# One core, a fused convolution and selective scan: a carry column is added one scan ahead of its use instead of two

## What is computed

```python
def step(h, inp):
    dt_t, B_t, C_t, x_t = inp
    dA = jnp.exp(dt_t[..., None] * A)
    dBx = dt_t[..., None] * B_t[:, None, :] * x_t[..., None]
    h = dA * h + dBx
    y = jnp.einsum('bdn,bn->bd', h, C_t)
    return (h, y)
```

## Time and profile before

| what | us |
|---|---|
| median of 3 runs | 13839.43 (13836.56 to 13845.37) |
| the profiled execution | 13837.79 |
| its span, first to last instruction | 13836.0 |
| VectorE busy | 13466.6 (97%) |
| GpSimd busy | 13246.6 (96%) |
| ScalarE busy | 12104.2 (87%) |
| TensorE busy | 10079.9 (73%) |

### The profile page before, as it was taken

How to read it: one execution, slowest core, us unless ns; L and a number is a source line. 1 busy time by engine, 2 the same in 40 slices (tenths; PEclk the granted TensorE clock), 3 DMA queues, 4 the chain that set the end, 5 groups by cost and what they waited for, 6 DMA issues and landing times.

```text
span 13836.0 us, 170380 instructions
## 1 busy us (share of the span) xinstructions
PE 10079.9 (73%) x34752; PEld 2897.7 (21%) x34752; DVE 13466.6 (97%) x12084; ACT 12104.2 (87%) x24809; POOL 13246.6 (96%) x3076
## 2 busy tenths in 40 slices
PE   6777777777777777777777777777777777777776
PEld 1222222222222222222222222222222222222221
DVE  7999999999999999999999999999999999999999
ACT  7888888888888888888988888888898888888888
POOL 6999999999999999999999999999999999999999
PEclk8888888888888888888878888788888888888887
DMA  6667676666766676666667666666666666666665
GB/s 146 161 154 161 155 163 156 158 157 157 164 156 160 152 163 158 160 157 156 158 159 164 153 163 151 163 159 156 161 153 163 156 161 156 160 156 163 158 155 128
DMA packets 1195180, 2175.99 MB, mean 157 GB/s; under 512 B 152321, under 2 KB 161594, under 8 KB 1194042
## 3 DMA queue, kind: packets, MB, share of 16 engines
q1 hardware_dynamic: 1192762, 2164.07, 66.7%
q10 hardware_dynamic: 1280, 0.02, 0.0%
HBM read 1811.17 MB, written 352.32 MB: 156 GB/s over the span
## 4 chain that ended last, share of the span: by engine, by line
POOL 53%; issue 32%; DVE 6%; ACT 5%; PE 1%; DMA 1%; SPq 0%; POOLq 0%; ACTq 0%; DVEq 0%
POOL hq L1064 38%; POOL dbx L1054 15%; DVE hq L946 4%; ACT ps_a L640 2%; DVE dbx L929 1%; ACT dbx L654 1%; DMA b_rep<-bc_d 0%; DMA dt_d<-dt 0%; DVE pp L905 0%; ACT xh L600 0%; ACT L600 0%; ACT L765 0%; PE ps_acc L456 0%; DMA dtx_d<-sp 0%; POOLq L1063 0%
## 5 line engine op out<-in xcount | busy, mean ns | idle before, releaser
L1064 POOL TENSOR_TENSOR hq<-hq,c_rep 128x2048 f32<-128x2048 f32 x2048 | 9251.0, 4535 | 468.8 <-ACT carry L659 465.0
L946 DVE TENSOR_TENSOR_SCAN hq<-ps_a,dbx 128x512 f32<-128x512 f32 x8192 | 9443.6, 1207 | 128.8 <-ACT dbx L654 47.2
L640 ACT ACTIVATE ps_a<-dt_rep,A_neg 128x512 f32<-128x512 f32 x8192 | 5625.2, 687 | 1294.7 <-DVE hq L946 1231.5
L1054 POOL TENSOR_TENSOR dbx<-dtx_rep,b_rep 128x2048 f32<-128x2048 f32 (+1 forms) x1024 | 4082.1, 3986 | 99.1 <-DMA dtx_rep<-dtx_d 89.1
L654 ACT ACTIVATE dbx<-ps_a,dbx,carry 128x1 f32<-128x1 f32 x7168 | 2504.9, 349 | 240.2 <-POOL dbx L1054 140.4
L929 DVE TENSOR_TENSOR dbx<-dtx_rep,ps_b 128x2048 f32<-128x2048 f32 (+1 forms) x1280 | 2626.7, 2052 | 9.5 <-PE ps_b L444 9.3
L456 PE MATMUL ps_acc<-hq,dsum 128*32 128x512 f32 x16384 | 2334.0, 643 | 292.6 <-POOL hq L1064 292.6
L382 PE MATMUL pp<-sq,w_b1T 128*128 128x512 f32 x512 | 531.1, 1141 | 1608.7 <-ACT sq L579 1608.7
L444 PE MATMUL ps_b<-dbl,bsel 41*128 41x512 f32 x2560 | 1587.3, 703 | 153.3 <-DVE dbx L929 97.7
L400 PE MATMUL pp<-x,W_taps 128*128 128x512 f32 x768 | 693.3, 1002 | 895.2 <-DVE x L900 531.4
L456 PEld LDWEIGHTS ps_acc<-hq,dsum 128*32 128x32 f32 x16384 | 355.9, 111 | 1865.7 <-issue 1046.5
(11 more groups left out here) (123 smaller groups left out, 10466.4 us busy)
## 6 DMA issues: line engine op xcount, KB each, us to landing
dtx_rep<-dtx_d SPq DMA_DIRECT2D x2048, 256.0 KB, 5.4
dt_rep<-dt_d SPq DMA_DIRECT2D x2048, 256.0 KB, 6.3
c_rep<-bc_d SPq DMA_DIRECT2D x1024, 256.0 KB, 4.7
xr<-in_x SPq DMA_DIRECT2D x704, 256.0 KB, 10.9
b_rep<-bc_d SPq DMA_DIRECT2D x2048, 64.0 KB, 5.5
dtx_d<-sp SPq DMA_DIRECT2D x256, 512.0 KB, 2.8
dt_d<-dt SPq DMA_DIRECT2D x256, 512.0 KB, 6.1
xin<-in_x SPq DMA_DIRECT2D x256, 256.0 KB, 10.2
```

Of the source, the lines that this page charges most:

```text
L640: A(ps_a[:, BANK[i], :], dt_rep[:, q // NQ, g, :], ACT.Exp, scale=A_neg[:, q // NQ, q % NQ, g:g + 1]).then_inc(exp_done, 1)
L946: v.tensor_tensor_scan(hq[:, q % HQ, g, :], ps_a[:, BANK[i], :], dbx[:, slot(q), g, :], 0.0, ALU.mult, ALU.add).then_inc(scan_done, 1)
L1054: g.tensor_tensor(dbx[:, slot(q), m:, :], dtx_rep[:, d, m:, :], b_rep[:, q % NQ // 2, :].unsqueeze(1).to_broadcast([P, DG - m, T]), ALU.mu ...
L1064: g.tensor_tensor(quad, quad, c_rep[:, c % 2, q % NQ, :].unsqueeze(1).to_broadcast([P, DG, T]), ALU.mult).then_inc(cmul_done, 1)
```

## The change

The step at which each tile's carry is added becomes a list that is worked out once. For the first tile of the odd groups (tiles 4, 12, 20 and 28, whose product GpSimd makes, of tile 12 a part of the group) it is step i-1, and for all others step i-2 as before. So in steps 3, 11, 19 and 27 two carries stand next to each other, and in steps 2, 10, 18 and 26 there is none. Tile 8 stays in the burst of step 5. The adds themselves and their waits are the same.

```diff
+IN_BURST = ACT_XZ + 3
+ADD_AT = [[i for i in range(2, NT + 2) if i != IN_BURST and u == (i - 1 if i % (2 * DG) == DG else i - 2)] for u in range(NT)]
 BY_DVE = (0, 2, 3, 4, 6)
...
-                    if u + 2 < NT:
-                        if c % CH and u != ACT_XZ + 1:
-                            add_carry(b, c, u + 2)
-                    elif c + 1 < end and (c + 1) % CH:
-                        add_carry(b, c + 1, u + 2 - NT)
+                    for i in ADD_AT[u]:
+                        if i < NT:
+                            if c % CH:
+                                add_carry(b, c, i)
+                        elif c + 1 < end and (c + 1) % CH:
+                            add_carry(b, c + 1, i - NT)
...
                         if c % CH:
-                            add_carry(b, c, u + 3)
+                            add_carry(b, c, IN_BURST)
```

## The result

The changed kernel takes 14191.1 us (median of 4 runs, 14190.6 to 14197.0), the kernel before 13839.5 us. The ratio is 1.0255, 95% interval 1.0237 to 1.0272: **352 us slower**. The forecast was 14190.

The account below looks back on a forecast made before the run. VectorE, with almost no slack, was taken as the bound. Seven chunks at 1.1 us plus tile 12's 0.89, 3 x 0.39 and 3 x 0.41 gave 11.0 us an image, 352 us over 32 images: 14190 us, range 14090 to 14290.

Parts of the forecast that it names:

- The bound: Whole kernel: VectorE busy 97% of the span, under half a microsecond slack per chunk, so waits before scans lengthen it almost one for one.
- Tile 4, a dead heat: Step 3: carry 4 ready 1.00 us after scan 2 ends, scan 4 due at 1.06 us, so cost nil.
- Tile 12: Carry behind decay 13 and any `pool_part`: 0.89 us lost in chunk 1, 0.39 in chunks 2 to 4, 0.41 in 5 to 7.
- What comes back in chunks 2 to 4: ScalarE, no longer held at tile 4, is 0.50 us sooner; taken off tile 12's loss, leaving 0.39 us each.
- GpSimd's extra room hides nothing: Whole kernel: GpSimd's added time in longer chunks saves nothing, since scans would not wait for it.
- Tiles 20 and 28: Carries behind `evac_conv` and `square`: scan 20 loses 0.88 us, scan 26 regains 0.20; together 1.1 us a chunk.
- The pitch of the scans: VectorE scans without a wait follow each other by 1.13 us, though each shows 1.20 us.
- The waits: VectorE's waits for `add_carry` grow from 123 (47.2 us) to some 670, by about 300 us.
- Nothing is regained: Rival, chance 0.08: each place pays its own delay in full, 15.6 us an image, 14337 us.
- A new wait for GpSimd: Rival, chance 0.08: later `keep_carry` delays GpSimd's product for the next odd group, 86 us on top, 14276 us.
- Faster: Rival, chance 0.04: ScalarE no longer stands still before a late GpSimd product with decay i+1 queued behind; 13783 us.
- My bound of 56 us: Most that rival "Faster" could gain: VectorE's 47.2 us of waits for `add_carry` plus 9 us uncounted idle time.

## Why the prediction was right, and where it was not

*The bound.* VectorE without slack, so that a delay ahead of a scan counts almost one for one: right. Its busy time is the same to 6 us, and the chunks grew by what their scans came late, less what waits further on swallowed.

*Tile 4, a dead heat.* Right in chunks 1 to 5 and 7: scan 4 loses 0.02 us or less. Wrong in chunk 6, which the sum left out: ScalarE comes late out of chunk 5 there, the carry had a lead of 0.35 us and not the 1.03 us of chunks 1 and 5, and scan 4 loses 0.19 us.

*Tile 12.* With `pool_part` scan 12 was forecast 1.12 us late, 0.89 us net of what scan 13 wins back, from a chunk whose lead was small (0.14 us; the average of chunk 1 is 0.27). Averaged over the images it is 1.00 us in chunk 1 and 0.9 us net. That the net figure is met is luck: in the very chunk of the rows it is 0.91 us and 0.7 net, and scan 9 had already won back 0.20 us there. In chunks 5 to 7 scan 12 loses 0.30 to 0.33 us for the 0.41 forecast. With tile 12 alone moved, chunk 6 does lose 0.41; in the changed kernel the carry of tile 4 is out of the way too, and that alone raises the lead at tile 12 of chunk 6 from 0.23 to 0.34 us.

*What comes back in chunks 2 to 4.* The mechanism is right, but the term was taken from one image. I took off 0.50 us. In that image chunk 2 wins back 0.53 us at scans 4, 9, 13 and 17, and grew by 1.50 us for the 1.49 forecast. The average is 0.8 us and 1.23 us, since in nine of the 32 images chunk 2 wins back 1.3 to 1.5 us, most of it at scan 9 (0.76 us) and scan 17 (0.45 us). There VectorE had waited for TensorE's sum in its product `y` and for ScalarE in its softplus instruction. Of 48 and 20 such waits in the whole kernel one each is left, at the very end and the very beginning of the span:

```profile
DVE y L916 <- PE ps_acc L456: 29.3, 48, 10.2
...
DVE pp L905 <- ACT sp L620: 21.3, 20, 15.3
```

```profile
DVE y L919 <- PE ps_acc L458: 10.2, 1, 10.2
...
DVE pp L908 <- ACT sp L622: 15.0, 1, 15.0
```

Why it is these images isn't shown. The sentence that GpSimd's extra room hides nothing was wrong for chunks 2 to 4: with tile 20 or 28 alone moved this room halves ScalarE's wait for GpSimd, and scans start sooner for it.

*Tiles 20 and 28.* 0.90 us at scan 20 for 0.88, and 0.49 us at scan 28 for the 0.46 that is 1.13 less 0.67; scans 22 to 27 win back 0.2 to 0.3 us. Chunks 4 and 5 are not as I took them. In chunk 4 the place costs 0.79 us at scan 28: two instructions of the attention stand ahead of the carry in step 25, and its lead was 0.05 us and not 0.35. In chunk 5 it costs 0.80 us, with a lead of 0.21, and scans 22 to 27 win back 0.54, because four small instructions of the attention had held scan 27. I had counted none of these.

*The pitch of the scans.* The 1.13 us for scans without a wait was read at scan 21 of the earlier trace rows, which the same paragraph reads as waiting for its carry. In the trace the commonest pitch of two scans is 1.11 us; the slip is under 0.02 us for a scan and changes no term by more than 0.03 us.

So the sum came out at 11.0 us for an image where 11.1 were measured, but that it is so close is in part luck: terms of +0.2 us each (chunks 4 and 6) and -0.3 us (chunk 2) cancel in it, and in chunk 5 two of 0.3 us. Tile 20 and, outside chunks 4 and 5, tile 28 were good to 0.03 us, tile 12 in chunks 1 and 5 to 7 to 0.1, the return in chunk 2 to 0.3, the sum by chunk to 0.3, and only the total to 0.1.

*The waits.* VectorE's waits were forecast at about 350 us and are 453: I gave the net loss, where the table counts the waits and not what is regained behind them.

*The rivals.* "Nothing is regained" (14337 us) fell: it would have been right only if scans 26 and 9 had not been waiting already. "A new wait for GpSimd" fell: its product is late 3 times in the changed kernel, 2.4 us in all, and its waits for `keep_carry`, longer by 329 us, held up no scan. "Faster" was the true mechanism at one place of four, worth 44 us by itself. My bound of 56 us held, but not by its working: it counted waits for a carry alone, and these gave 9 us.

## What to carry to other kernels

In this kernel a carry came as late as all that stood between it and its scan in ScalarE's order, so "one step later" is no unit: before a carry is moved, list what the steps that it crosses hold, by pitch and not by duration, and set that against its lead over its reader. Move it only where the lead is larger or where the wait that it gets out of the way is longer; here that was one tile of four. Work the sum out on more than one image when the chunks of the kernel before differ from image to image. And where several engines are nearly full, look which is next: here ScalarE's gain at tile 4 ended at 0.3%, with GpSimd and VectorE both busy for more than 99% of chunk 3.

## What the runs showed that was not expected

Pitch, and not duration, decided each place. With sums of durations tile 20's carry would have come 0.68 + 0.58 = 1.26 us behind the start of decay 21, and tile 28's 1.94 us behind that of decay 28; measured were 1.09 and 1.70. The idle time in front of a scan is short by the overlap of two scans, 0.07 to 0.09 us: scan 20 starts 0.90 us later and shows 0.81 us idle.

A longer chunk is in part its own remedy: each of the three moves that made the kernel slower also shortened ScalarE's waits for GpSimd, so that their costs could not be added.
